# A graph kernel's gathers of edge rows: a wait on the gather two places back instead of one pause per group

## The reference: what is computed

```python
# layer 0, feat = norm(x), edge_feat = edge_attr_64
feat_n = feat * norm_out[:, None]
agg_h = jax.ops.segment_sum(feat_n[src], dst, num_segments=N)
agg_e = jax.ops.segment_sum(edge_feat, dst, num_segments=N)
# layer 1, embeddings = norm(x), edge_val = edge_weight
messages = edge_val[:, None] * embeddings[edge_src]
neighbor_emb = jax.ops.segment_sum(messages, edge_dst, num_segments=embeddings.shape[0])
```

## Time and profile before

| | us |
|---|---|
| three runs | 2355.99, 2357.14, 2359.45 |
| the profiled execution | 2355.14 |
| its span in the trace | 2353.1 |

### The profile page before, as it was taken

One profiled execution on the slowest core, in us unless ns is written; L12 is line 12 of the kernel. 1 busy time (PEld: TensorE's weight loads), 2 busy tenths in 40 slices (PEclk: granted clock), 3 DMA queues, 4 the chain that ended last, 5 costly groups with the idle time before them and its releaser, 6 DMA issues. The chain is left out here.

```text
span 2353.1 us, 35048 instructions
## 1 busy us (share of the span) xinstructions
PE 1849.0 (79%) x10583; PEld 1437.1 (61%) x10584; DVE 1246.6 (53%) x3264; ACT 710.1 (30%) x1624; POOL 911.5 (39%) x933
## 2 busy tenths in 40 slices
PE   6589668666465899999975998768888684799976
PEld 5355446444253799999962565535656472688875
DVE  6644676766456444444458556633443376333345
ACT  5222333333342122112127931122222132133324
POOL 0555555555320222222220435555655300254542
PEclk9999889888777799999996999969999897799997
DMA  7544444444264011011113323333333317211224
GB/s 228 143 120 123 127 113 113 117 109 111 77 271 164 27 32 33 31 34 35 35 46 126 104 92 103 95 102 95 103 102 103 95 55 303 107 62 64 64 58 148
DMA packets 171236, 239.46 MB, mean 102 GB/s; under 512 B 74145, under 2 KB 139261, under 8 KB 168692
## 3 DMA queue, kind: packets, MB, share of 16 engines
q0 software_dynamic: 42336, 112.74, 16.7%
q1 hardware_dynamic: 116884, 113.45, 14.8%
q10 hardware_dynamic: 11904, 11.96, 1.6%
HBM read 184.86 MB, written 56.12 MB: 102 GB/s over the span
## 5 line engine op out<-in xcount | busy, mean ns | idle before, releaser
L655 POOL DMA_INDIRECT agg_message<-table,edges_src x638 | 626.8, 982 | 617.3 <-DMA agg_message<-table,edges_src 264.2
L2822 PEld LDWEIGHTS ex_p_h<-ex_xT,ex_own_up 128*128 128x128 f32 (+1 forms) x2464 | 281.3, 192 | 2.7 <-issue 1.4
L2822 PE MATMUL ex_p_h<-ex_xT,ex_own_up 128*128 128x128 f32 (+1 forms) x2464 | 282.0, 276 | 1.0 <-DVE ex_xT L2873 1.0
L714 PE MATMUL agg_partial<-agg_message,moe_up 128*64 128x321 f32 x638 | 124.6, 533 | 117.0 <-issue 95.8
L2877 DVE COPY ex_own_up<-moe_up 128x1280 f32 x114 | 100.5, 883 | 168.7 <-PE ex_p_h L2822 167.9
L2781 POOL DMA_INDIRECT ex_x<-moe_in,route_token_at x58 | 57.4, 989 | 311.9 <-PE ex_p_x L2812 242.3
L714 PEld LDWEIGHTS agg_partial<-agg_message,moe_up 128*64 128x64 f32 x638 | 53.0, 161 | 163.3 <-issue 144.0
L714 PE MATMUL agg_partial<-agg_message,agg_onehot 128*64 128x256 f32 x638 | 97.2, 446 | 66.0 <-issue 55.3
L726 ACT COPY agg_span<-agg_partial 128x321 f32<-128x321 f32 (+1 forms) x108 | 43.2, 400 | 336.4 <-PE agg_partial L718 286.7
L2865 ACT ACTIVATE ex_gate_h<-ex_p_h 128x640 f32<-128x640 f32 x56 | 39.5, 705 | 315.3 <-PE ex_p_h L2822 315.3
L3018 ACT COPY ex_own_up<-moe_up 128x1024 f32 x66 | 67.5, 1044 | 213.4 <-PE ex_p_h L2991 163.2
(11 more groups left out here) (665 smaller groups left out, 3684.0 us busy)
## 6 DMA issues: line engine op xcount, KB each, us to landing
moe_up<-in_f_w SPq DMA_DIRECT2D x8, 1386.0 KB
agg_message<-in_edge_rows SPq DMA_DIRECT2D x54, 192.0 KB
agg_message<-table,edges_src POOLq DMA_INDIRECT x638
sums<-agg_span SPq DMA_DIRECT2D x107, 80.2 KB
moe_up<-in_f_w SPq DMA_DIRECT2D x4, 2048.0 KB, 15.3
moe_down<-in_f_w SPq DMA_DIRECT2D x4, 2048.0 KB
sums<-agg_span SPq DMA_DIRECT2D x107, 64.0 KB
moe0b_down<-in_f_w SPq DMA_DIRECT2D x8, 768.0 KB
```

What stands on the lines that cost most here:

```text
L655: pool.indirect_dma_start(out=to[:, k * w:k * w + D], out_offset=None, in_=self.table, in_offset=bass.IndirectOffsetOnAxis(ap=self.edges.s ...
L714: mm = pe.matmul(self.partial[h * W:(h + 1) * W, 0:w], hot[:, k * W:(k + 1) * W], msg[:, k * w:(k + 1) * w], start=(k % RUN == 0), stop=(g ...
L2822: return pe.matmul(to, own_up[:, o:o + n], xT[:, k * D + c * P:k * D + (c + 1) * P], start=(c == 0), stop=(c == 1))
```

## The change

POOL no longer waits at the start of a group for the whole group before. Ahead of each gather it waits for the gather two places in front of it, across the groups' borders too: gather n of a group (n from 0) uses semaphore `gathered[n % 2]`, one for the even and one for the odd gathers of the layer, and waits until all earlier gathers on that semaphore have landed. Thus at most two gathers are in flight. PE waits for the counts of both semaphores. The `used` wait stays.

```diff
-        self.gathered, self.featured = ([m.sem(f"{n}{k}") for k in range(ring)] for n in ("gathered", "featured"))
+        self.gathered, self.featured = ([m.sem(f"{n}{k}") for k in range(c)] for n, c in (("gathered", 2), ("featured", ring)))
...
-    def landed(self, pool, g, n):
-        pool.wait_ge(self.gathered[g % self.ring], (g // self.ring * GE + n) * 16)
+    def count(self, g, n):
+
+        return (g * RUN + n // 2) * 16
 
     def gather(self, pool, g):
         if g >= self.ring:
             pool.wait_ge(self.used, g - self.ring + 1)
         to, w = self.slot(self.message, g, self.width), self.width
-        if g:
-            self.landed(pool, g - 1, len(self.tiles(g - 1)))
-        for k in self.tiles(g):
+        for n, k in enumerate(self.tiles(g)):
             t = self.place(g) + k
+            before = self.count(g, n)
+            if before:
+                pool.wait_ge(self.gathered[n % 2], before)
             pool.indirect_dma_start(out=to[:, k * w:k * w + D], out_offset=None, in_=self.table,
                                     in_offset=bass.IndirectOffsetOnAxis(ap=self.edges.src[:, t:t + 1], axis=0))\
-                .then_inc(self.gathered[g % self.ring], 16)
+                .then_inc(self.gathered[n % 2], 16)
...
-        pe.wait_ge(self.gathered[g % self.ring], (g // self.ring * GE + len(tiles)) * 16)
+        for k in range(2):
+            pe.wait_ge(self.gathered[k], self.count(g, len(tiles) + 1 - k))
```

## The result

The change makes the kernel slower by 0.6%: 2371.45 us (median of nine runs, 2364.68 to 2375.52) against 2356.59 us (nine runs, 2352.32 to 2359.45), ratio 1.0061 with a 95% interval of 1.0047 to 1.0075. Slower was right. The profiled execution has a span of 2369.9 us, 16.8 more than before.

A forecast was written before the change was run, and what follows sets the result against it. The prediction took POOL's chain of six gathers and the last one's round trip as the bound; +66.8 us in layer 0 and +42.8 us in layer 1 made +109.6 us, forecast 2465 us, range 2405 to 2510.

The forecast's parts named there:

- What bounds the kernel: End of both layers: POOL issues six gathers, waits for the last one's round trip, issues six more; its pace sets time.
- the two stretches: Gathers from layer 0's second group, and from layer 1's barrier, to the last full group's last: 540.1 and 471.7 us before.
- The failed step: POOL's gathers: the round trip, taken from one gather plus one pause, is 3.90 us in layer 0, 3.66 in layer 1.
- the prediction's own formula: Each stretch takes its steps times half a round trip: 311 × 3.903 / 2 = 606.9 us, 281 × 3.662 / 2 = 514.5 us.
- the 0.95 that was forecast: Slack of a pair of gathers on POOL, 3.45 − 2.5 = 0.95 us, which takes up delays of late gathers.
- The floor: Rival: trips fall nearly to the shortest, 3.45 us, in both layers; +9 us or less; everything up to +40 us 6%.
- The wait is never felt: Rival: POOL's waking hides behind the gather in between, a gather is ready every 1.25 us; 2204 us, chance 5%.
- PE then sets the pace: In the faster rival, PE can give back at most its unnamed waits, 95.8 + 55.3 us, so the time is 2204 us.
- Break-even at a pause of 2.44 us: The change gains only if POOL's mean pause falls below 2.44 us, where 296 × (0.98 + pause) equals before's 1011.8 us.
- At nothing: Layer 0's first group and layer 1's first six groups come later but cost nothing, hidden by the barriers behind them.

The follow-up runs named there:

- a_two: The changed kernel with the `used` wait repeated ahead of each gather, so that landing waits stand in an instruction of their own; 2467.37 us, ratio 1.0460.
- experiment 7: The changed kernel's wait two places back, landing wait in the gather itself, ahead of only every second, every third or a group's first gather; ratios 0.9841, 0.9800, 1.0025.
- b_nopause: The kernel before without the wait for the group before, so that only the ring slot holds a group back; 2394.50 us, ratio 1.0169.
- d3: The changed kernel with three semaphores, each gather waiting for the one three places in front; 2374.63 us, ratio 1.0062.
- a_swap: The changed kernel with the landing wait first and the `used` wait second at a group's first gather; 2343.48 us, ratio 0.9934.
- a_pair: The changed kernel with the wait two places back only ahead of every second gather, landing wait in the gather itself; ratio 0.9841.

## Why the prediction was wrong

*What bounds the kernel* was right. The chain on POOL sets the time late in both layers: exchanging two of its waits alone gave 31 us, and the changed kernel's +18.4 us in the two stretches gave +16.8 us of span.

*The failed step* is "in layer 0 0.980 + 2.923 = 3.90 us [...] in layer 1 0.987 + 2.675 = 3.66 us [...] That is the full round trip: descriptors, transfer, landing and POOL's waking." It took the waking behind a wait of one kind (in an instruction of its own, 1.10 us) for that behind the other (in the gather, 0.62 us), because it read the trip from pauses that nearly all have the first kind. In the changed kernel five of six gathers have the other kind. Measured for groups 8 to 52, mean start to start two places apart, by place in the group:

```
              n=0    n=1    n=2    n=3    n=4    n=5    mean   a group takes
layer 0       4.07   3.76   3.23   3.32   3.19   3.43   3.50   10.51 (10.46 before)
layer 1       3.79   3.61   3.39   3.39   3.18   3.36   3.45   10.34 (10.13 before)
a_two, lay. 0 4.16   3.80   3.76   3.84   3.71   3.98   3.88   11.66
a_two, lay. 1 3.95   3.70   3.74   3.76   3.66   3.91   3.79   11.32
```

With the trip that was forecast for layer 0, 3.90, six gathers take 11.7 us, and a_two, where every landing wait is of the slow kind, has 11.66. With 3.50 and 3.45 the prediction's own formula gives 311 × 3.50 / 2 = 544 us and 281 × 3.45 / 2 = 485 us, +4 and +13; measured were +6.8 and +11.6. The formula, the number of steps and the stretches stand; the trip was too long by 0.40 and 0.21 us, of which the waking is about 4/6 × 0.48 = 0.32 (n = 1 follows n = 0 and shares its slow waking). The 0.08 us left in layer 0 fits the mean landing, which is 0.09 us shorter there. In layer 1 some 0.1 us of delays came on top; what they are was not tried.

*Why slower at all, then?* Where nothing interferes, both orders take about the same: five issues of 1.25 and 3.45 us are 9.7 us before, and 3.05 + 3.05 + 3.5 = 9.6 us now; the medians of a group are 10.35 and 10.38 us in layer 0, and 9.83 and 9.81 in layer 1. But the means rise, by 0.05 and 0.21 us. Before, one landing in six could hold up POOL when it came late; now each can, and a pair has 3.05 − 2.5 = 0.55 us of slack, not the 0.95 that was forecast. That is argued from the rows, but the series of experiment 7 fits it: with the same waking, waiting ahead of every second gather (0.9841) instead of each (0.9934) saves some 22 us.

*The floor* (+9 us, or up to +40) is what came, and had 6%. It was reached for another reason than the one given: not because the delays went, but because the waking was shorter. That the time fell there is no merit of the argument given for it. Its lower end was set too high as well, since 3.45 us was not the least trip.

*The wait is never felt* did not come: 434 of the changed kernel's 638 gathers have idle time ahead of them that a landing ends, 402.4 us in all, against 95 before. Its price rested on the step that "PE then sets the pace; it can give back at most" 151 us. That fails as well: with no landing wait (b_nopause) PE's idle time before the products fell by 138.5 us, and the program took 37 us more. *Break-even at a pause of 2.44 us* was right: the measured trips, less a gather, are 2.52 and 2.46 us, just above it, and the change cost 0.6%.

*At nothing:* layer 0's second group starts at 81.50 instead of 81.69, so that its first group costs nothing, as forecast. Layer 1's first six groups cost nothing either. Its first gather starts 6.2 us later, which is layer 0's delay, and the barrier ends only 4.2 us later (1389.70 against 1385.49), with POOL still standing 18.93 us at it. The first gathers, before and changed:

```profile
1306.00 0.99 POOL L655 DMA_INDIRECT agg_message<-table,edges_src  x1 [75.12 <-DMA table<-layer_XN]
...
1312.24 0.99 POOL L657 DMA_INDIRECT agg_message<-table,edges_src  x1 [75.07 <-DMA table<-layer_XN]
```

## What to carry to other kernels

A wait costs by where it stands: when an instruction needs two, put the one that comes last in the instruction itself (here the one written first in the code) and the one long met in front. That alone was worth 31 us of 2357. Before a pause is taken from a trace as the price of a wait that will stand elsewhere, look for every form in which the trace already has it, and compare the shortest of each form; the means mix them. Take away waits on a gathering queue by degrees and watch who waits next: in the series here one wait in two or three gathers was best, and none was worst.

## What was not expected of the hardware

- POOL starts a gather 0.62 us after the last completion write of the gather that it waits for, or 1.10 us after it if the wait is an instruction of its own ahead of the gather; 233 cases of the first and 86 of the second in the changed kernel, 90 of the second in before.
- A gather of 128 rows of 1 KB has its last completion write 2.43 to 2.50 us after its start, in the median, with two, three or six in flight.
- With gathers 1.25 us apart and no pause, PE's semaphore updates became visible up to 11.0 us after PE's end (d3), where 0.04 us is usual; with no more than two gathers in a row there was no case over 1 us in some 80 of each of three kernels (changed, a_swap, a_pair). The cause stays open.
